# A transformer layer with eight experts: the experts' rows in 63 whole and 9 half units that the chip plans, instead of 80 fixed chunks

## The chip, the cores and the metric

The kernel runs on one core of a Trainium2 chip. The metric is the time of one execution on the device in microseconds (us), lower is better. The kernel before has a median of 3489.76 us over 3 runs (3483.92 to 3495.27).

## What is computed

The layer takes 32 sequences of 512 tokens with 256 features, all in float32:

```python
x = layernorm(x + attention(x))       # 16 heads of 16, softmax over 512 keys, projection, bias
x = layernorm(x + experts(x))
# experts: 16384 tokens, 8 experts, each token goes to its best 2
cap = int(N * K * CF / E)             # 5120 rows at most for one expert
logits = x @ Wg.T
top_v, top_i = top_k(logits, 2); gates = softmax(top_v)
pos = cumsum(onehot(top_i)) - 1; keep = pos < cap
h = rows_of_expert @ W1[e]            # 256 -> 1024
h = gelu(h[:, :512]) * h[:, 512:]
y = h @ W2[e]                         # 512 -> 256
out = segment_sum(gate * y, token)
```

There are 16384 * 2 = 32768 rows to compute, which is 64 times 512. How they fall on the eight experts depends on the data.

## The kernel before

The program has three blocks, one after the other, each ended by a barrier of all engines.

**Attention** (`attention`) goes over the 32 sequences in a software pipeline that is written out in full. Beside the heads it normalises, computes the router's logits, and gives each token two slots in a table in HBM, `expert_rows`: 8 experts times 5120 slots, 260 numbers wide (256 features, and the token's number, its gates and its first expert). POOL scatters the rows into their slots with indirect DMAs (L504). The table was filled before with blank rows, whose token number is far out of range. The running number of rows of each expert is `carry`. When the last iteration is over, ACT and DVE split the weights of expert 0 into a high and a low part (L778, L1022), beside the last scatter.

**Experts** (`experts`) goes over 80 chunks of 512 slots, ten for each expert, full or blank, whatever the data are, in loops of the program (`chunks`). TensorE multiplies float32 as three products of high and low parts. For a chunk:

- SP loads the rows, transposed in four quarters, and their meta data (`load_rows`, five DMAs, L1134 and L1135), two buffers deep. It does so once DVE has turned the rows that lay in the buffer and has read their meta data (`s_turn`, `s_meta`).
- DVE turns the rows (L1280), ACT and DVE split them (L1231, L1286).
- PE computes the hidden products f = 0 to 3 (`hidden`, L1193, 12 matmuls of 512 columns each), and between f = 1 and f = 2 the output products of the chunk before (`output`, L1206, 48 matmuls of 256 columns).
- ACT applies the Gelu (L1235), DVE multiplies (`product`, L1292), ACT and DVE split the result (L1241, L1297), ACT scales the output by the gate (`scale`, L1249), and POOL adds the rows into the result in HBM with four indirect DMAs (L1163).
- DVE reads gate and token out of the meta data (`meta`, L1309 to L1313).

Once per expert, in its second chunk, SP loads the next expert's raw W1 (four DMAs of 256 KB, L226) and W2 (one of 512 KB, L227) into one raw buffer, and POOL splits them (L1176, L1178) into the other of two sets of split weights, `w1_hi`, `w1_lo`, `w2_hi`, `w2_lo` (named stack and w_buf in the trace).

**final_norm** normalises the result, limited by its loads and stores.

Of the kernel before, what the change touches and what calls it, by code (L numbers as in the profile page):

```python
# [10 lines left out]

# [115 lines left out]
def settle(engine, sem):  # L127


    engine.sem_inc(sem, 1)  # L130
# [72 lines left out]
LOADED = 16 * (QUARTERS + 1)  # L203
W_PIECES = 3


class Weights:
# [3 lines left out]
    def __init__(self, stacks, w2_buf, probs, w1, w2):  # L211
# [12 lines left out]
    def load(self, engine, e, s_raw):  # L224
        for a in range(QUARTERS):
            engine.dma_start(self.raw1[a * BLOCK:(a + 1) * BLOCK], self.w1_rows[e, a]).then_inc(s_raw, 16)  # L226
        engine.dma_start(self.raw2, self.w2_rows[e]).then_inc(s_raw, 16)  # L227

    def pieces(self, par):

        return [(self.raw1[:, 0], self.w1_hi[par][0], self.w1_lo[par][0]),
                (self.raw1[:, 1], self.w1_hi[par][1], self.w1_lo[par][1]),
                (self.raw2, self.w2_hi[par], self.w2_lo[par])]


def attention(nc, x, w_qkv, w_proj, b_proj, w_gate, x1_dram, table, stacks, probs, weights):
# [3 lines left out]
    cap = table.shape[0] // EXPERTS  # L240
# [7 lines left out]
    with ExitStack() as ctx:  # L248
# [77 lines left out]
        token = sb("token", [P, TILES])  # L326

# [34 lines left out]
        s_raw = sem("s_raw_a")  # L362
        s_whi, s_wlo = sem("s_whi_a"), sem("s_wlo_a")
# [11 lines left out]
        def _(sp):  # L375
# [8 lines left out]
            def body(it):  # L384
                b = it.b
                for s in range(4):
# [36 lines left out]
                    if s == 3 and it.known and b == n_seq:  # L423
                        sp.wait_ge(s_pv, n_seq * UNITS)
                        weights.load(sp, 0, s_raw)
# [10 lines left out]
            sp.wait_ge(s_fill, 16 * EXPERTS * per)  # L436
# [3 lines left out]
        def _(pool):  # L440
# [25 lines left out]
            pool.wait_ge(s_pad, 2 * GROUPS)  # L466
            pool.wait_ge(s_weights, 64)

            def body(it):
# [26 lines left out]
                if it.on(-2):  # L496
                    pool.wait_ge(s_slot, b - 1)

                    pool.wait_ge(s_fill, (b - 1) * (16 * EXPERTS) if it.filling else 16 * EXPERTS * per)
                    settle(pool, s_waited_pool)  # L500
                    for k in range(TOPK):
                        for t in range(TILES):
                            c = k * TILES + t
                            pool.indirect_dma_start(  # L504
                                table, bass.IndirectOffsetOnAxis(ap=slot[:, c:c + 1], axis=0), row[it.odd][:, t, :], None,
                                bounds_check=table.shape[0] - 1, oob_is_err=False).then_inc(s_scatter, 16)
# [27 lines left out]
        def _(pe):  # L534
# [157 lines left out]
            iterations(pe, n_seq, body)  # L692

        @block.scalar
        def _(act):
# [79 lines left out]
            act.wait_ge(s_raw, LOADED)  # L775
            act.wait_ge(s_cols, n_seq * ALL)
            for raw_w, hi, _ in weights.pieces(0):
                act.copy(hi, raw_w).then_inc(s_whi, 1)  # L778

        @block.vector  # L780
        def _(dve):
# [238 lines left out]
            for i, (raw_w, hi, lo) in enumerate(weights.pieces(0)):  # L1020
                dve.wait_ge(s_whi, i + 1)
                dve.tensor_tensor(lo, raw_w, hi.bitcast(F32), ALU.subtract).then_inc(s_wlo, 1)  # L1022


def experts(nc, table, weights, x1_dram):

    cap = table.shape[0] // EXPERTS
    per = cap // SEQ
    n_chunks = EXPERTS * per
    n_tokens = x1_dram.shape[0]
    assert cap % SEQ == 0 and per % 2 == 0 and EXPERTS % 2 == 0 and EXPERTS > 4 and per > 2
    WIDTH = DIM // QUARTERS  # L1040
    chunk_x = table[:, 0:DIM].rearrange("(n b j) (a c) -> n a j b c", b=SEQ // BLOCK, j=BLOCK, a=QUARTERS)
    chunk_meta = table[:, DIM:ROW].rearrange("(n t p) c -> n p t c", p=P, t=TILES)

    with ExitStack() as ctx:
# [12 lines left out]
        quarters = [sb(f"quarters{i}", [P, SEQ // BLOCK, WIDTH]) for i in range(2)]  # L1057
        meta_rows = [sb(f"meta_rows{i}", [P, TILES, ROW - DIM]) for i in range(2)]
        turned = sb("turned", [P, KT, SEQ])
        x_hi = [sb(f"x_hi{i}", [P, KT, SEQ], F32R) for i in range(2)]  # L1060
        x_lo = [sb(f"x_lo{i}", [P, KT, SEQ], F32R) for i in range(2)]
        w1_hi, w1_lo, w2_hi, w2_lo = weights.w1_hi, weights.w1_lo, weights.w2_hi, weights.w2_lo
# [8 lines left out]
        expert_no = sb("expert_no", [P, 1])  # L1071

        s_rows = [sem(f"s_rows{i}") for i in range(2)]
        s_raw = sem("s_raw")
        s_whi = sem("s_whi")
        s_w = sem("s_w")
# [13 lines left out]
        s_eno = sem("s_eno")  # L1090


        s_waited_sp, s_waited_pool = sem("s_waited_sp_e"), sem("s_waited_pool_e")

        ADDED = 16 * TILES

        class Chunk:


            def __init__(self, e, par, lead, half, odd, last=False):  # L1100
                self.e, self.par, self.lead, self.half, self.odd, self.last = e, par, lead, half, odd, last
                self.n = half * 2 + odd
                self.first = isinstance(half, int) and self.n == 0
                self.final_expert = isinstance(e, int) and e == EXPERTS - 1

        def chunks(engine, body):

            halves = per // 2

            def expert(e, par, final=False):  # L1110
                for odd in range(2):
                    body(Chunk(e, par, True, e * halves, odd))
                with engine.Fori(1, halves - 1 if final else halves) as i:
                    for odd in range(2):
                        body(Chunk(e, par, False, e * halves + i, odd))
                if final:
                    for odd in range(2):
                        body(Chunk(e, par, False, e * halves + halves - 1, odd, last=True))

            expert(0, 0)  # L1120
            expert(1, 1)
            with engine.Fori(1, EXPERTS // 2 - 1) as pair:
                expert(pair * 2, 0)
                expert(pair * 2 + 1, 1)
            expert(EXPERTS - 2, 0)
            expert(EXPERTS - 1, 1, final=True)
# [3 lines left out]
        @block.sync  # L1130
        def _(sp):
            def load_rows(odd, n):
                for a in range(QUARTERS):
                    sp.dma_start(quarters[odd][a * BLOCK:(a + 1) * BLOCK], chunk_x[n, a]).then_inc(s_rows[odd], 16)  # L1134
                sp.dma_start(meta_rows[odd][:], chunk_meta[n]).then_inc(s_rows[odd], 16)  # L1135

            load_rows(0, 0)
            load_rows(1, 1)

            def body(k):  # L1140
                if k.lead and k.odd and not k.final_expert:
                    wait(sp, s_w, k.e * W_PIECES)
                    settle(sp, s_waited_sp)
                    weights.load(sp, k.e + 1, s_raw)
                if not k.last:
                    sp.wait_ge(s_turn, k.n * KT + KT)
                    settle(sp, s_waited_sp)
                    sp.wait_ge(s_meta, k.n + 1)
                    settle(sp, s_waited_sp)
                    load_rows(k.odd, k.n + 2)  # L1150

            chunks(sp, body)
            sp.wait_ge(s_add, n_chunks * ADDED)

        @block.gpsimd
        def _(pool):
            def add_out(buf, n):

                pool.wait_ge(s_scaled, n * TILES + TILES)
                wait(pool, s_add, n * ADDED)  # L1160
                settle(pool, s_waited_pool)
                for t in range(TILES):
                    pool.indirect_dma_start(  # L1163
                        x1_dram, bass.IndirectOffsetOnAxis(ap=token[buf][:, t:t + 1], axis=0), out[buf][:, t, :], None,
                        bounds_check=n_tokens - 1, oob_is_err=False, compute_op=ALU.add).then_inc(s_add, 16)

            def body(k):
                if not k.first:
                    add_out(1 - k.odd, k.n - 1)
                if k.lead and k.odd and not k.final_expert:  # L1170

                    pool.wait_ge(s_raw, k.e * LOADED + LOADED)
                    wait(pool, s_out, k.e * per)
                    settle(pool, s_waited_pool)
                    for i, (raw, hi, lo) in enumerate(weights.pieces(1 - k.par)):
                        pool.tensor_copy(hi, raw).then_inc(s_whi, 1)  # L1176
                        pool.wait_ge(s_whi, k.e * W_PIECES + (i + 1))
                        pool.tensor_tensor(lo, raw, hi.bitcast(F32), ALU.subtract).then_inc(s_w, 1)  # L1178

            chunks(pool, body)  # L1180
            add_out((n_chunks - 1) % 2, n_chunks - 1)

        @block.tensor
        def _(pe):
            def hidden(c, f):

                wait(pe, s_mul, c.n * FT + (f - 1))
                for part in range(2):
                    cols = slice(part * FF + f * P, part * FF + (f + 1) * P)
                    i = 0  # L1190
                    for k in range(KT):
                        for w, xx in ((w1_hi, x_hi), (w1_lo, x_hi), (w1_hi, x_lo)):
                            last = pe.matmul(ps_hid[f % 2][:, part, :], w[c.par][k][:, cols], xx[c.odd][:, k, :],  # L1193
                                             start=i == 0, stop=i == 3 * KT - 1)
# [3 lines left out]
            def output(par, buf, n):  # L1198
# [282 lines left out]
```

## Time and profile before

| | |
|---|---|
| median of 3 runs | 3489.76 us (3483.92 to 3495.27) |
| profiled execution | 3492.51 us |
| its span, from the first to the last instruction | 3490.8 us |
| attention, up to the first row load of the experts | 0 to 2002.18 us |
| experts | 2002.18 to 3389.01 us |
| final norm | 3389.01 to 3490.8 us |
| PE, DVE, ACT, POOL busy, share of the span | 92%, 70%, 61%, 50% |

An instruction's time is its own duration on its engine. Matmuls overlap, so the time of one matmul in a row of them is the distance between starts, and not the duration shown. The value in brackets behind a row of the timeline is the idle time of the engine before it, and what ended it. The execution profiled took 2.75 us more than the median.

### The profile page before, as it was taken

What the parts mean: (1) busy time and instruction counts of PE and PEld (TensorE: products, weight loads), DVE (VectorE), ACT (ScalarE), POOL (GpSimd) and SP (SyncE); (2) the same over time, 40 slices, a digit from 0 to 9 for tenths busy, and PEclk for the clock granted to TensorE, in tenths of its full rate; (3) what the DMA queues carried; (4) which work ended last, traced back from release to release, by engine and by line L of the source; (5) the groups of instructions that cost most, each with busy time, mean ns of one, the idle gap of its engine ahead of it and who ended that gap; (6) DMA issues with size and microseconds to landing.
All of it is one profiled execution on the core that took longest, in us unless ns stands there. A gap on an engine that the chain in (4) does not pass through costs nothing. (4 is left out here: it accounts for less than half of the span.)

```text
span 3490.8 us, 65927 instructions
## 1 busy us (share of the span) xinstructions
PE 3226.1 (92%) x22018; PEld 2115.3 (61%) x22018; DVE 2446.6 (70%) x5673; ACT 2113.1 (61%) x4197; POOL 1755.3 (50%) x1501
## 2 busy tenths in 40 slices
PE   5999999999999999999999599999999999999960
PEld 3444444444444445444444288888888888888850
DVE  4888888888888888888887364545455545454439
ACT  2788888888877787878886444444444444444420
POOL 5356565656556565656562343434353534353334
PEclk7999999999999999999998799999999999999985
DMA  2455555433333333333332244434345434442439
GB/s 87 142 160 173 160 173 160 123 87 98 87 97 82 97 88 98 87 96 91 92 94 65 77 75 63 74 58 77 57 68 78 62 61 62 70 61 43 62 73 338
DMA packets 397883, 339.88 MB, mean 97 GB/s; under 512 B 257720, under 2 KB 315456, under 8 KB 397632
## 3 DMA queue, kind: packets, MB, share of 16 engines
q1 hardware_dynamic: 334656, 252.20, 27.8%
q0 software_dynamic: 58368, 67.74, 11.3%
q10 hardware_dynamic: 4608, 16.78, 1.2%
q8 instruction: 136, 2.23, 0.3%
q14 instruction: 115, 0.94, 0.1%
HBM read 89.92 MB, written 152.17 MB: 69 GB/s over the span
## 5 line engine op out<-in xcount | busy, mean ns | idle before, releaser
L974 DVE TENSOR_REDUCE peak<-ps 128x1 f32<-128x512 f32 x2048 | 1338.5, 683 | 293.0 <-PE ps L654 292.4
L749 ACT ACTIVATE probs<-ps 128x512 f32<-128x512 f32 x2048 | 1124.5, 611 | 173.8 <-PE ps L664 164.9
L1163 POOL DMA_INDIRECT x<-out,token x320 | 501.7, 1568 | 800.0 <-ACT out L1249 669.4
L1193 PE MATMUL ps_hid<-x_hi,stack 128*128 128x512 f32 x2560 | 804.2, 395 | 30.9 <-DVE x_lo L1286 26.3
L664 PE MATMUL ps<-stack 50*128 50x512 f32 x2048 | 786.2, 453 | 3.4 <-DVE peak L974 2.7
L654 PE MATMUL ps<-stack 48*128 48x512 f32 x2048 | 753.8, 446 | 18.9 <-DMA stack<-qk_lo 13.6
L1292 DVE TENSOR_TENSOR hid<-ps_hid,act_in 128x512 f32<-128x512 f32 x320 | 219.1, 689 | 598.0 <-ACT act_in L1235 597.8
L654 PEld LDWEIGHTS ps<-stack 48*128 48x128 f32 x2048 | 336.0, 189 | 466.7 <-issue 223.2
L1193 PEld LDWEIGHTS ps_hid<-x_hi,stack 128*128 128x128 f32 x2560 | 476.5, 188 | 140.3 <-DVE x_lo L1286 26.4
L680 PE MATMUL ps_pv<-probs,v 128*17 128x512 f32 x4096 | 546.9, 606 | 1.2 <-ACT probs L749 1.2
L1193 PE MATMUL ps_hid<-x_lo,stack 128*128 128x512 f32 x1280 | 505.4, 395 | 0.0
L1206 PE MATMUL ps_out<-w_buf,h_hi 128*128 128x256 f32 x2560 | 463.7, 283 | 2.9 <-DVE h_lo L1297 2.9
L504 POOL DMA_INDIRECT expert_rows<-row,slot x256 | 254.9, 996 | 407.9 <-DVE token L954 323.6
L1206 PEld LDWEIGHTS ps_out<-w_buf,h_hi 128*128 128x128 f32 x2560 | 401.8, 189 | 10.1 <-issue 3.3
L1235 ACT ACTIVATE act_in<-ps_hid 128x512 f32<-128x512 f32 x320 | 190.2, 597 | 308.6 <-PE ps_hid L1193 308.6
L664 PEld LDWEIGHTS ps<-stack 50*128 50x128 f32 x2048 | 335.4, 186 | 58.6 <-DVE peak L974 38.7
L1206 PE MATMUL ps_out<-w_buf,h_lo 128*128 128x256 f32 x1280 | 363.1, 284 | 0.0
L488 POOL TENSOR_TENSOR qk<-qk 128x512 f32<-128x512 f32 x128 | 164.0, 1281 | 355.0 <-ACT qk L700 355.0
L1249 ACT ACTIVATE out<-ps_out,gate 128x256 f32<-128x256 f32 x320 | 125.7, 476 | 274.2 <-PE ps_out L1206 274.2
L1193 PEld LDWEIGHTS ps_hid<-x_lo,stack 128*128 128x128 f32 x1280 | 241.1, 188 | 57.0
L1297 DVE TENSOR_TENSOR h_lo<-hid,h_hi 128x512 fp32r<-128x512 f32 x320 | 237.8, 747 | 15.2
L1206 PEld LDWEIGHTS ps_out<-w_buf,h_lo 128*128 128x128 f32 x1280 | 241.9, 189 | 0.0
(136 smaller groups left out, 4095.6 us busy)
## 6 DMA issues: line engine op xcount, KB each, us to landing
stack<-qk_hi SPq DMA_DIRECT2D x1024, 64.0 KB, 2.3
expert_rows<-blank SPq DMA_DIRECT2D x80, 520.0 KB, 4.0
quarters<-expert_rows SPq DMA_DIRECT2D x320, 128.0 KB, 2.7
stack<-qk_lo SPq DMA_DIRECT2D x512, 64.0 KB, 2.3
xs<-in_L_attn_x SPq DMA_DIRECT2D x32, 512.0 KB, 4.3
x<-row SPq DMA_DIRECT2D x32, 512.0 KB, 3.3
fy<-x SPq DMA_DIRECT2D x32, 512.0 KB, 4.6
out<-fz ACTq DMA_DIRECT2D x32, 512.0 KB, 4.7
```

Source lines behind the costliest of these rows:

```text
L504: pool.indirect_dma_start(table, bass.IndirectOffsetOnAxis(ap=slot[:, c:c + 1], axis=0), row[it.odd][:, t, :], None, bounds_check=table.sh ...
L654: pe.matmul(ps[it.bank(("rows", n))][:], q_stack[s][part, h, t * P:(t + 1) * P], k_stack[s][part, h, :], start=True, stop=True).then_inc(s ...
L664: pe.matmul(ps[it.bank(("cols", n))][:], k_stack[g][part, h, t * P:(t + 1) * P], q_stack[g][part, h, :], start=True, stop=True).then_inc(s ...
L680: last = pe.matmul(ps_pv[32 * h:32 * h + HD + 1, :], v[par][:, t, HG * g + h, :], probs[:, (HG * t + h) % RING, :], start=t == 0, stop=t = ...
L749: act.activation(probs[:, j % RING, :], ps[it.bank(("cols", s * UNITS + j))][:], ACT.Exp, scale=SCALE).then_inc(s_exp, 1)
L974: dve.tensor_reduce(peak[s % 2][:, u:u + 1], ps[it.bank(("rows", n))][:], AX.X, ALU.max, negate=True).then_inc(s_max, 1)
L1163: pool.indirect_dma_start(x1_dram, bass.IndirectOffsetOnAxis(ap=token[buf][:, t:t + 1], axis=0), out[buf][:, t, :], None, bounds_check=n_t ...
L1193: last = pe.matmul(ps_hid[f % 2][:, part, :], w[c.par][k][:, cols], xx[c.odd][:, k, :], start=i == 0, stop=i == 3 * KT - 1)
L1206: last = pe.matmul(ps_out[:, t, :], hh[buf][:, f, t * P:(t + 1) * P], w[par][:, f, :], start=i == 0, stop=i == 3 * FT - 1)
L1235: act.activation(act_in[f % 2][:], ps_hid[f % 2][:, 0, :], ACT.Gelu).then_inc(s_gelu, 1)
L1292: dve.tensor_tensor(hid[f % 2][:], ps_hid[f % 2][:, 1, :], act_in[f % 2][:], ALU.mult).then_inc(s_mul, 1)
L1297: dve.tensor_tensor(h_lo[c.odd][:, f, :], hid[f % 2][:], h_hi[c.odd][:, f, :].bitcast(F32), ALU.subtract).then_inc(s_hlo, 1)
```

## The change

The experts' work is cut into units instead of chunks: 63 whole ones of 512 slots and then 9 halves of 256. That is the number that suffices for any distribution of 32768 rows on eight experts. Which slots and which expert's weights belong to a unit is worked out at the end of attention: PE sums `carry` over the partitions, and DVE works out two numbers for each unit (`plan.numbers`: place in the table, expert) and the expert for the gates (`plan.expert`), in some 70 instructions on tiles of up to 544 numbers a partition. A unit without work gets a blank place added behind the table. SP reads a number into a register (`value_load`, a TENSOR_LOAD) ahead of a load of rows or weights.

Since any unit may have another expert than the one before, **W1 and W2 are loaded and split for every unit**. ACT makes the high parts and DVE the low ones, in pieces of 128x1024 between the steps of a unit; POOL only adds rows. The buffers of rows become three. The loops of the program become code written out.

```diff
+class Plan:
+    def __init__(self, sb, n_tokens, cap):
+        self.per = cap // SEQ
+        self.blank = EXPERTS * self.per
+        halves = n_tokens * TOPK // (SEQ // 2) + EXPERTS - 1
+        self.whole = (halves - EXPERTS) // 2
+        self.n_halves = halves - 2 * self.whole
...
+    def rows(self, engine, n):
+        return engine.value_load(self.numbers[0:1, 0, n:n + 1], min_val=0, max_val=last)
+    def weights(self, engine, n):
+        return engine.value_load(self.numbers[0:1, 1, n:n + 1], min_val=0, max_val=EXPERTS - 1)
...
@@ attention, sync @@
-                    if s == 3 and it.known and b == n_seq:
-                        sp.wait_ge(s_pv, n_seq * UNITS)
-                        weights.load(sp, 0, s_raw)
+            sp.wait_ge(s_pv, n_seq * UNITS)
+            sp.wait_ge(s_planned, 2)
+            first = plan.weights(sp, 0)
+            weights.load_w1(sp, first)
+            weights.load_w2(sp, first)
@@ attention, tensor @@
+            pe.matmul(ps_pv[:, 0:EXPERTS], ones[:], carry[:], start=True, stop=True).then_inc(s_total, 1)
@@ attention, scalar @@
-            for raw_w, hi, _ in weights.pieces(0):
-                act.copy(hi, raw_w).then_inc(s_whi, 1)
@@ experts, sync @@
-            def body(k):
-                if k.lead and k.odd and not k.final_expert:
-                    wait(sp, s_w, k.e * W_PIECES)
-                    weights.load(sp, k.e + 1, s_raw)
-                if not k.last:
-                    sp.wait_ge(s_turn, k.n * KT + KT)
-                    sp.wait_ge(s_meta, k.n + 1)
-                    load_rows(k.odd, k.n + 2)
+            for n in range(RING_X):
+                load_rows(n)
+            expert = plan.weights(sp, 1)
+            sp.wait_ge(s_w1, KT)
+            weights.load_w1(sp, expert)
+            for n in range(n_units):
+                if n + RING_X < n_units:
+                    sp.wait_ge(s_turn, n * KT + KT)
+                    sp.wait_ge(s_meta, n + 1)
+                    load_rows(n + RING_X)
+                if n + 2 < n_units:
+                    later = plan.weights(sp, n + 2)
+                    sp.wait_ge(s_w1, (n + 2) * KT)
+                    weights.load_w1(sp, later)
+                if n + 1 < n_units:
+                    sp.wait_ge(s_w2, n + 1)
+                    weights.load_w2(sp, expert)
+                    expert = later
@@ experts, gpsimd: the split of the weights goes @@
-                        pool.tensor_copy(hi, raw).then_inc(s_whi, 1)
-                        pool.tensor_tensor(lo, raw, hi.bitcast(F32), ALU.subtract).then_inc(s_w, 1)
@@ experts, scalar @@
+            for n in range(n_units):
+                more = n + 1 < n_units
+                if more:
+                    high_x(n + 1)
+                gelu(n, 0)
+                gelu(n, 1)
+                high_h(n, 0)
+                if more:
+                    high_w1(n + 1, 0)
+                high_h(n, 1)
+                if more:
+                    high_w1(n + 1, 1)
+                high_w2(n)
+                if n:
+                    scale(n - 1)
+                gelu(n, 2)
+                gelu(n, 3)
+                high_h(n, 2)
+                high_h(n, 3)
@@ experts, vector: as on ACT, with turn and low_x, then @@
+                product(n, 0)
+                product(n, 1)
+                low_h(n, 0)
+                if more:
+                    low_w1(n + 1, 0)
+                low_h(n, 1)
+                if more:
+                    low_w1(n + 1, 1)
+                low_w2(n)
+                meta(n)
+                product(n, 2)
...
```

The two places where instructions move are these. On SP, the loads of one chunk in the middle of an expert before (quarters and meta_rows are the buffers of the rows, probs is the raw buffer of the weights; ISA rows write a register):

```order
L1134 ISA
L1134 DMA quarters<-expert_rows 32x16x64
L1134 ISA
L1134 DMA quarters<-expert_rows 32x16x64
L1134 ISA
L1134 DMA quarters<-expert_rows 32x16x64
L1134 ISA
L1134 DMA quarters<-expert_rows 32x16x64
L1135 ISA
L1135 DMA meta_rows<-expert_rows 128x4x4
```

and now those of one whole unit (the three quarters' and two weights' DMAs left out read like their neighbours):

```order
L256 TENSOR_LOAD plan_numbers
L256 ISA x2
L1258 ISA
L1258 DMA quarters<-expert_rows 32x16x64
...
L1260 ISA
L1260 DMA meta_rows<-expert_rows 128x4x4
L259 TENSOR_LOAD plan_numbers
L259 ISA x2
L228 ISA
L228 DMA probs<-in_L_ffn_W 32x2x1024
...
L231 ISA
L231 DMA probs<-in_L_ffn_W 128x4x256
```

Five loads a chunk have become ten a unit, with two reads of a number into a register ahead of them. On DVE, one chunk before, from the turn of the next rows on:

```order
L1280 STREAM_TRANSPOSE turned<-quarters 128x512 x2
L1286 TENSOR_TENSOR x_lo<-turned,x_hi 128x512 x2
L1292 TENSOR_TENSOR hid<-ps_hid,act_in 128x512 x2
L1297 TENSOR_TENSOR h_lo<-hid,h_hi 128x512 x2
L1309 SCALAR_TENSOR_TENSOR gate_part<-meta_rows,expert_no 128x4
L1312 TENSOR_TENSOR gate<-gate_part,meta_rows 128x4
L1313 COPY token<-meta_rows 128x4
L1292 TENSOR_TENSOR hid<-ps_hid,act_in 128x512 x2
L1297 TENSOR_TENSOR h_lo<-hid,h_hi 128x512 x2
```

and one whole unit now:

```order
L1397 STREAM_TRANSPOSE turned<-quarters 128x512 x2
L1403 TENSOR_TENSOR x_lo<-turned,x_hi 128x512 x2
L1417 TENSOR_TENSOR hid<-ps_hid,act_in 128x512 x2
L1422 TENSOR_TENSOR h_lo<-hid,h_hi 128x512
L1408 TENSOR_TENSOR stack<-probs,stack 128x1024
L1422 TENSOR_TENSOR h_lo<-hid,h_hi 128x512
L1408 TENSOR_TENSOR stack<-probs,stack 128x1024
L1412 TENSOR_TENSOR w_buf<-probs,w_buf 128x1024
L1431 SCALAR_TENSOR_TENSOR gate_part<-meta_rows,plan_expert 128x4
L1434 TENSOR_TENSOR gate<-gate_part,meta_rows 128x4
L1435 COPY token<-meta_rows 128x4
```

Three subtractions of 128x1024 stand ahead of the reading of the meta data, for which SP waits.

## Rows read from the trace of the kernel before

**Rows 1.** The page: span, and busy time of each engine.

```profile
span 3490.8 us, 65927 instructions
...
PE 3226.1 (92%) x22018; PEld 2115.3 (61%) x22018; DVE 2446.6 (70%) x5673; ACT 2113.1 (61%) x4197; POOL 1755.3 (50%) x1501
```

**Rows 2.** Windows: stretch, length, busy times, granted clock, DMA share, GB/s.

```profile
2009.83:3363.77 1353.94, 1349.37 (x7632) 1175.88 (x7632) 707.24 (x1201) 583.90 (x1112) 574.57 (x356) 1.00 0.42 64
...
2603.15:2620.14 16.99, 16.99 (x98) 14.86 (x97) 8.20 (x17) 7.34 (x14) 6.25 (x5) 1.00 0.43 62
...
2688.00:2705.00 17.00, 17.00 (x98) 14.80 (x98) 8.64 (x17) 7.45 (x14) 6.28 (x5) 1.00 0.72 139
...
3363.77:3388.00 24.23, 7.47 (x48) 7.29 (x48) 1.98 (x3) 3.29 (x7) 9.73 (x7) 0.73 0.12 13
```

**Rows 3.** Timeline of one chunk: start, us, engine, line, what, count, [idle before].

```profile
2605.93 0.40 PE L1206 MATMUL ps_out<-w_buf,h_hi 128*128 128x256 f32 x2
...
2606.29 0.40 PE L1206 MATMUL ps_out<-w_buf,h_hi 128*128 128x256 f32 x2
...
2609.08 0.17 DVE L1313 COPY token<-meta_rows 128x4 uint32<-128x4 uint32 x1
...
2609.50 1.92 SPq L1134 DMA_DIRECT2D quarters<-expert_rows  x4
...
2611.97 1.57 ACT L1249 ACTIVATE out<-ps_out,gate 128x256 f32<-128x256 f32 x4 [3.87 <-PE ps_out L1206]
...
2615.30 0.69 DVE L1292 TENSOR_TENSOR hid<-ps_hid,act_in 128x512 f32<-128x512 f32 x1 [6.05 <-ACT act_in L1235]
```

**Rows 4.** SP's queue in the second chunk of an expert.

```profile
2694.31 1.91 SPq L1134 DMA_DIRECT2D quarters<-expert_rows  x4
...
2697.16 1.82 SPq L226 DMA_DIRECT2D probs<-in_L_ffn_W  x4
...
2699.16 0.39 SPq L227 DMA_DIRECT2D probs<-in_L_ffn_W  x1
```

**Rows 5.** DMA issues, 2050 to 3360 us: count, KB each, median us to landing.

```profile
quarters<-expert_rows SPq DMA_DIRECT2D x304, 128.0 KB, 2.7
...
probs<-in_L_ffn_W SPq DMA_DIRECT2D x24, 256.0 KB, 4.5
...
probs<-in_L_ffn_W SPq DMA_DIRECT2D x6, 512.0 KB, 6.4
```

**Rows 6.** Timeline of the end of attention and the start of the experts.

```profile
1983.53 0.19 DVE L911 TENSOR_TENSOR pos_all<-count,ps 128x32 f32<-128x32 f32 x1 [0.30 <-PE ps L641]
...
1985.26 1.04 ACT L778 CAST w_buf<-probs 128x1024 fp32r<-128x1024 f32 x1
...
1985.73 2.35 DVE L1022 TENSOR_TENSOR stack<-probs,stack 128x1024 fp32r<-128x1024 f32 x2
...
1996.75 0.97 POOL L504 DMA_INDIRECT expert_rows<-row,slot  x1 [0.30 <-issue]
...
2002.18 1.92 SPq L1134 DMA_DIRECT2D quarters<-expert_rows  x4
...
2009.83 1.22 PE L1193 MATMUL ps_hid<-x_hi,stack 128*128 128x512 f32 x2 [26.33 <-DVE x_lo L1286]
...
2019.84 0.60 ACT L1235 ACTIVATE act_in<-ps_hid 128x512 f32<-128x512 f32 x1 [0.81 <-PE ps_hid L1193]
```

**Rows 7.** Timeline of the end of the experts.

```profile
3369.63 0.63 PE L1206 MATMUL ps_out<-w_buf,h_hi 128*128 128x256 f32 x2
...
3370.27 0.63 PE L1206 MATMUL ps_out<-w_buf,h_hi 128*128 128x256 f32 x2
...
3373.84 0.29 PE L1206 MATMUL ps_out<-w_buf,h_lo 128*128 128x256 f32 x1
...
3376.61 1.55 POOL L1163 DMA_INDIRECT x<-out,token  x1 [8.69 <-ACT out L1249]
...
3378.47 1.55 POOL L1163 DMA_INDIRECT x<-out,token  x1 [0.30 <-issue]
```

More of the change, by code:

```diff
@@ L1019, in _, with planned, then @@
             iterations(dve, n_seq, body)
[L1020 to L1037, printed above, removed]
+            def planned(ins):
+                ins.then_inc(s_plan, 1)
+                step[0] += 1
+            def then():
+                dve.wait_ge(s_plan, step[0])
@@ new lines, in _ @@
+            total = work([P, EXPERTS])
+            reached = work([P, EXPERTS, per])
+            own_chunks = work([P, EXPERTS])
+            own_steps = work([P, EXPERTS])
+            small = work([P, EXPERTS])
+            small_at = work([P, EXPERTS])
+            upto = work([P, 2 * EXPERTS, EXPERTS])
+            ends = work([P, 2 * EXPERTS])
+            ended = work([P, plan.n_chunks, EXPERTS])
+            start = work([P, plan.n_chunks])
+            chunk_e = work([P, plan.n_chunks])
@@ new lines, in _ @@
+            then()
+            planned(dve.tensor_reduce(own_chunks, reached, AX.X, ALU.add))
+            then()
+            planned(dve.tensor_tensor(small, own_steps, own_chunks, ALU.subtract))
+            then()
+            for e in range(EXPERTS):
+                planned(dve.tensor_copy(upto[:, e, 0:e + 1], own_chunks[:, 0:e + 1]))
+                planned(dve.tensor_copy(upto[:, EXPERTS + e, 0:e + 1], small[:, 0:e + 1]))
+            planned(dve.scalar_tensor_tensor(small_at, number[:], float(per), own_chunks, ALU.mult, ALU.add))
@@ new lines, in _ @@
+            dve.tensor_scalar(plan.numbers[:, 1, 0:W], chunk_e[:, 0:W], EXPERTS - 1.0, None, ALU.min).then_inc(s_planned, 1)
+            then()
+            planned(dve.tensor_reduce(start, ended, AX.X, ALU.max))
+            planned(dve.scalar_tensor_tensor(place, chunk_e, float(per), chunk_no[:], ALU.mult, ALU.add))
+            then()
+            planned(dve.tensor_tensor(place, place, start, ALU.subtract))
+            then()
+            planned(dve.tensor_scalar(place, place, float(plan.blank), None, ALU.min))
@@ L1089, in experts, with cols, scaled_before, added_before @@
         s_add = sem("s_add")
[L1090 to L1126, printed above, removed]
+        def cols(n):
+            return plan.tiles(n) * P
+        def scaled_before(n):
+            return plan.tiles_before(n)
+        def added_before(n):
+            return 16 * plan.tiles_before(n)
         block = ctx.enter_context(nc.Block())
@@ L1155, in _ @@
+            sp.wait_ge(s_add, added_before(n_units))
         @block.gpsimd
         def _(pool):
[L1157 to L1162, printed above, removed]
+            for n in range(n_units):
+                pool.wait_ge(s_scaled, scaled_before(n + 1))
+                wait(pool, s_add, added_before(n))
+                for t in range(plan.tiles(n)):
```

374 lines of the change are left out of this document (225 added, 149 removed).

## The prediction

> **What bounds the kernel now.** I read the page first, for the engines' shares: PE is busy for 92% of the span [rows 1]. The windows then show the experts' stage apart. From its first matmul at 2009.83 us to the end of the last hidden products at 3363.77 us, PE is busy for 1349.37 of 1353.94 us at a granted clock of 1.00 [rows 2], while DVE has 707 and ACT 584 us of work. A chunk takes 16.99 us, of which DVE is busy for 8.20 and ACT for 7.34. So this stage is bound by PE, and there are 80 chunks of it. The timeline shows what a chunk is made of: its output products start at 2605.93, and three matmuls of 256 columns take 0.36 us, so 0.12 us each [rows 3]. 48 of these take 5.76 us, which leaves 11.2 us for the 48 hidden ones of 512 columns, 0.234 us each. A chunk whose rows belong to nobody costs PE as much as a full one. The attention and the final norm are not touched, and I leave them at their times.
>
> **Fewer units: 288.8 us less.** 63 whole units take the place of the first 63 of 80 chunks. If PE stays the bound, each of the 17 chunks that go gives back 16.99 us: 17 x 16.99 = 288.8 us. The half units have to be added to that, below.
>
> **Does the new work fit into a whole unit?** Each now splits 1.5 MB of weights. ACT gets three copies of 128x1024, of 1.04 us each, 3.1 us in all; DVE three subtractions, two of which took 2.35 us, so 3.6 us in all [rows 6]. ACT comes to 10.5 us and DVE to 11.8 us of 16.99. The order matters more than the sum. Both engines do the splits while PE works on the output products. ACT stands idle for 3.87 us there before it scales, and DVE for 6.05 us before its next product [rows 3]. The 3.1 and 3.6 us fit into these gaps, so I cost them at nothing in a whole unit. If that cover went, each microsecond over it would cost 62 us. DVE's reading of the meta data, which ends at 2609.25 (8.9 us after the chunk's start, with 24 hidden matmuls ahead of the output at 2605.93), moves to 12.5 us, because the three subtractions are ahead of it.
>
> **The loop of loads.** That reading is what SP waits for, and behind SP's wait now stand the weights of the next units too. There is one raw buffer, so the weights go round in a loop, for W2 in this order: the reading ends; SP issues 0.25 us later (2609.25 to 2609.50, [rows 3]); a number is read into a register, r; five loads of rows are issued in 2.5 us; a second number, r; W1's four loads go 2.0 us ahead of W2's; W2 lands 6.4 us after its issue [rows 4, 5]; ACT's copy 1.0, DVE's subtraction 1.2, the reading 0.55, and 0.1 for the handings over. That makes 14.0 us + 2r. By W1, landing after 4.5 us with three copies and a Gelu half's split behind it, the sum is the same within 0.2 us.
>
> No row shows r. Nearest from below is SP's issue of one load, 0.39 us [rows 4]; even nothing is possible. From above, a whole small load lands after 2.7 us [rows 5]. I take r = 0.8, nearer to an issue, since four bytes have no queue of packets ahead. The Trainium skill, page "DMA: Bandwidth & Descriptors", section "Latency and other measured facts", gives a floor of about 600 ns for such a read; by that floor the loop would be 0.4 us shorter and the whole time about 3 us. With mine the loop is 15.6 us. In a whole unit that is under 16.99 us, so PE hides it with 1.4 us to spare; r above 1.5 us, or as much more in the landing, would end that.
>
> **The half units are bound by the loop: 122.6 us more.** PE needs 72 matmuls of 256 columns, 72 x 0.12 = 8.6 us. The splits and loads of weights don't get smaller, and the loop stays at 15.6 us. So in the halves PE waits for DVE's low part of the weights and for products queued behind it. Counted from the end of the whole units' hidden products: the first half unit, whose weights were loaded under a whole one, reads its meta data after 10.7 us (an estimate: 12.5 less what the narrower steps save); six loops of 15.6 us are 93.6; one without rows to load is 15.6 - 2.5 - 0.8 = 12.3; one with W2 alone is 0.25 + 6.4 + 2.75 less some queue, 9.1; product and splits 2.0; the last output products, 24 matmuls at the lower clock, 5.1. Together 133 us. Before, the output products ended 10.4 us after the hidden ones (3363.77 to 3374.13, [rows 7]). So 133 - 10.4 = 122.6 us are added. PE's pauses also lower its clock: after the wait at the end three matmuls take 0.64 instead of 0.36 us, mean clock 0.73 [rows 2, 7]. A whole half unit at that rate, 1.2 GHz, is 72 x 0.213 = 15.3 us, just under the loop; I cost it at nothing.
>
> **The start: 3.0 us more.** The plan has some 30 dependent steps on DVE. In the routing ten such steps lie between 1983.53 and 1985.73 [rows 6], 0.22 us each, so 6.6 us. Four of them are on 544 numbers, and a product on 512 takes 0.69 us [rows 3], so 2 us more; 34 small copies without a wait between them I put at 0.1 us each. That is about 12 us from 1985.7, so to 1998. Beside it POOL scatters until 1997.7 and the block ends at 2002.18 [rows 6]. So the plan is hidden with a small margin; without it up to 12 us would show. ACT's and DVE's splits of the first weights move behind the barrier: two copies and two subtractions, 3.3 us with their overlap. The first matmul comes 7.65 us after the first row load there [rows 6], and most of that is waiting for the rows, so they are hidden. The first read adds r = 0.8 us. Then SP has three sets of rows to issue, 3 x (2.5 + 0.8), before W1 of unit 1, which lands at about 2019; ACT's third Gelu, at 2019.84 before [rows 6], comes at 2022.6 instead, for 2.2 us. POOL makes three small index tiles at the very start of the program, before it has anything to split; I cost them at nothing, and at some tenths if nothing covers them.
>
> **The end: 4.5 us less.** The last unit has two tiles, not four: 0.8 us less scaling of 1.57 [rows 3], and two adds fewer at 1.86 us from start to start [rows 7].
>
> **The sum.** -288.8 + 122.6 + 3.0 - 4.5 = -167.7 us. The span goes from 3490.8 to 3323 us, the profiled time from 3492.5 to 3325 us. The median of before is 2.75 us under that execution, so I say **3322 us**.
>
> **The rivals.**
> - *As above*: 60%, 3295 to 3360 us by itself (r from 0 to 1.5 and as much in the landing; at the clock's lower level some microseconds per half unit).
> - *Loads are quicker than the rows say, and the halves run at PE's pace.* Nine times 8.64 and the tails are 86 us instead of 133, so 3275 us. For it: the landings in rows 5 were measured with five loads just ahead and adds beside them, and half units have half of these. Against it: W2 is always behind W1, and DVE alone has at least 8.20 / 2 + 3.6 = 7.7 us of work in a half unit. 10%. The Trainium skill, same page, section "Anatomy of one DMA", fits 2.0 us + bytes / 436e3 for a DMA of GpSimd alone, which would be 3.2 us for W2. By that rule the halves' loop is 12.4 us and the time about 3299 us; row 5's 6.4 us speaks against it.
> - *The loop is over 17 us and binds the whole units too.* The DMA engines go from a share of 0.43 to 0.72 in the window with one load of weights [rows 2], and now every unit is such a window. Each microsecond of loop over 16.99 costs 62 us there and 7 more in the halves; a loop of 18 us gives 3322 + 62 x 1.0 + 7 x 2.4 = 3401 us. Against it: the 6.4 us were measured in such windows. 25% from 3340 to 3480 us.
> - *Slower.* The same mechanism decides the sign at a loop of 19.4 us, where 62 x 2.4 + 7 x 3.8 = 175 us eat the gain: W2 would have to land after 10.2 instead of 6.4 us, or r be at its upper bound of 2.7. With 20 us: 3539 us. 5%.
> - That half units cost PE as much as whole ones is excluded by the output products, which run at 256 columns in half the time.
>
> **How the numbers follow.** The forecast is the likeliest case. The range reaches down to the quick loads, 3275, and up to a loop of 18 us, 3400; the upper part of the third case and the fourth stay out, with what lies below. A measurement of this kernel can tell about 0.3%, 10 us, from no change. Faster by more: 94%; slower by more: 5%; within: 1%.
>
> **What would show it.** Right: 63 periods of 16.9 to 17.0 us with clock 1.00; a third stretch of some 130 us with PE half idle, released by DVE's products; in it 15 to 16 us from one row load of SP to the next; SP's W2 landing at 6 to 7 us; first matmul 27 us after the end of routing, not more. Wrong: periods of over 17 us in the whole units with ACT's copy of probs released by a DMA (rivals three and four), or 9 to 10 us in the halves (rival two).

## The result and the profile after

| | before | after |
|---|---|---|
| median, same chip | 3490.16 us (3483.92 to 3495.27, 4 runs) | 3410.75 us (3407.68 to 3413.28, 4 runs) |
| ratio, 95% interval | | 0.977 (0.9755 to 0.9784) |
| span profiled | 3490.8 | 3410.2 |
| first experts' matmul | 2009.83 | 2013.95 |
| from there to the end of the last output products | 1364.3 | 1279.6 |
| from there to the final norm's first load | 14.9 | 8.4 |
| final norm | 101.8 | 108.3 |

The change gains 2.3%, 79 us, which is less than half of the 168 us that were forecast. It was forecast at 3322 us, with a range up to 3400, so it lies 11 us outside. The profiled executions differ by 80.6 us: the first matmul comes 4.1 us later, the stage is 84.7 us shorter, the wait behind it 6.5 us shorter, and the norm 6.5 us longer. The loss against the forecast is in the experts' stage. The windows of after, of whole units and of half units (the columns as in [rows 2]):

```profile
2050.00:3050.00 1000.00, 947.50 (x5319) 809.81 (x5318) 632.25 (x997) 552.14 (x940) 367.27 (x223) 1.00 0.70 147
3150.00:3290.00 140.00, 95.23 (x650) 93.64 (x648) 70.14 (x156) 61.82 (x133) 33.84 (x22) 0.83 0.55 119
```

PE, which had no pause in a chunk before [rows 2], is idle for 5% of the whole units though its clock is 1.00. From one of ACT's copies of W2 to the next pass 18.04 us, the mean over 60, where a chunk took 16.99. In the halves a unit takes 16.2 to 18.0 us. The waits from 2050 to 3050 us (engine, tile, line, who is waited for: us in total, times, longest) say who holds it:

```profile
DVE stack L1408 <- ACT stack L1341: 271.8, 55, 6.1
ACT stack L1341 <- DMA probs<-in_L_ffn_W: 257.1, 55, 5.9
...
PE ps_hid L1302 <- DVE hid L1417: 52.3, 49, 2.1
...
ACT w_buf L1345 <- DMA probs<-in_L_ffn_W: 2.1, 4, 1.0
```

In every unit ACT's first copy of W1 waits for the weights, 4.7 us on average; DVE's low part waits for ACT, and PE for the product that is queued behind. It is W1 that is late: W2 is waited for in 4 units only. The timeline of one unit of after shows the loop (as [rows 3]; some rows of SP, ACT, DVE and POOL):

```profile
2500.26 0.16 DVE L1435 COPY token<-meta_rows 128x4 uint32<-128x4 uint32 x1
...
2500.54 1.55 POOL L1288 DMA_INDIRECT x<-out,token  x1 [10.42 <-ACT out L1363]
2501.22 2.02 SPq L1258 DMA_DIRECT2D quarters<-expert_rows  x4
...
2504.56 1.81 SPq L228 DMA_DIRECT2D probs<-in_L_ffn_W  x4
...
2506.13 1.69 POOL L1288 DMA_INDIRECT x<-out,token  x1 [0.30 <-issue]
...
2506.55 0.39 SPq L231 DMA_DIRECT2D probs<-in_L_ffn_W  x1
...
2512.96 1.05 ACT L1341 CAST stack<-probs 128x1024 fp32r<-128x1024 f32 x1 [4.55 <-DMA probs<-in_L_ffn_W]
...
2515.72 1.05 ACT L1345 CAST w_buf<-probs 128x1024 fp32r<-128x1024 f32 x1 [0.23 <-DMA probs<-in_L_ffn_W]
...
2518.39 0.16 DVE L1435 COPY token<-meta_rows 128x4 uint32<-128x4 uint32 x1
...
2519.34 1.92 SPq L1258 DMA_DIRECT2D quarters<-expert_rows  x4
```

The four parts of the loop, as means over 53 whole units, beside the terms of the forecast (the last one is what is left of its sum):

| part of the loop | forecast, us | measured, us |
|---|---|---|
| end of DVE's reading of the meta data (its copy of the token) to the rows' first issue: SP reads a number | 0.25 + 0.8 | 0.81 |
| rows' first issue to W1's first issue | 2.5 + 0.8 | 3.57 |
| W1's first issue to ACT's first copy | 1.5 + 4.5 | 8.07 (7.08 to 9.34) |
| ACT's first copy to the end of the meta reading | 5.25 | 5.6 |
| sum | 15.6 | 18.05 |

### The profile page after: what moved, and what is told of

Read it like the earlier page. It is cut to its first block and busy times, and to the rows that moved or that the text cites. A ratio compares the mean times of both kernels' runs of the same rounds, so it can differ in the third digit from the quotient of the medians.

```text
span 3410.2 us, 63298 instructions
## 1 busy us (share of the span) xinstructions
PE 3043.8 (89%) x21035; PEld 1947.2 (57%) x21035; DVE 2537.0 (74%) x5828; ACT 2217.3 (65%) x4280; POOL 1618.4 (47%) x1412
## 5 line engine op out<-in xcount | busy, mean ns | idle before, releaser
L1302 PE MATMUL ps_hid<-x_hi,stack 128*128 128x512 f32 (+1 forms) x2304 | 707.8, 391 | 131.5 <-DVE hid L1417 101.4
L1302 PE MATMUL ps_hid<-x_lo,stack 128*128 128x512 f32 (+1 forms) x1152 | 446.9, 388 | 0.0
L1408 DVE TENSOR_TENSOR stack<-probs,stack 128x1024 fp32r<-128x1024 f32 x144 | 175.8, 1222 | 354.4 <-ACT stack L1341 354.4
L1316 PE MATMUL ps_out<-w_buf,h_hi 128*128 128x256 f32 x2160 | 387.5, 281 | 1.9 <-DVE h_lo L1422 1.9
L1341 ACT CAST stack<-probs 128x1024 fp32r<-128x1024 f32 x144 | 150.9, 1048 | 345.9 <-DMA probs<-in_L_ffn_W 324.4
L1316 PEld LDWEIGHTS ps_out<-w_buf,h_hi 128*128 128x128 f32 x2160 | 336.7, 189 | 7.5 <-issue 2.1
L1316 PE MATMUL ps_out<-w_buf,h_lo 128*128 128x256 f32 x1080 | 303.5, 281 | 0.0
L1417 DVE TENSOR_TENSOR hid<-ps_hid,act_in 128x512 f32<-128x512 f32 (+1 forms) x288 | 184.2, 653 | 122.1 <-ACT act_in L1349 121.5
L1349 ACT ACTIVATE act_in<-ps_hid 128x512 f32<-128x512 f32 (+1 forms) x288 | 160.6, 574 | 136.9 <-PE ps_hid L1302 136.4
L750 ACT COPY qk<-ps 128x512 f32<-128x512 f32 x256 | 137.5, 589 | 132.5 <-PE ps L640 128.5
```

The costliest lines, as they stand in the source:

```text
L1302: last = pe.matmul(ps_hid[f % 2][:, part, 0:cols(n)], w[n % 2][k][:, w_cols], xx[n % 2][:, k, 0:cols(n)], start=i == 0, stop=i == 3 * KT - 1)
L1316: last = pe.matmul(ps_out[:, t, :], hh[n % 2][:, f, t * P:(t + 1) * P], w[n % 2][:, f, :], start=i == 0, stop=i == 3 * FT - 1)
L1408: dve.tensor_tensor(w1_lo[n % 2][k], raw1[:, k], w1_hi[n % 2][k].bitcast(F32), ALU.subtract).then_inc(s_w1, 1)
L1417: dve.tensor_tensor(hid[f % 2][:, 0:cols(n)], ps_hid[f % 2][:, 1, 0:cols(n)], act_in[f % 2][:, 0:cols(n)], ALU.mult).then_inc(s_mul, 1)
```

## The experiments

The theories after the result: **the loop**, as in the table, binds every unit (the rows in front of the weights, DVE's meta reading behind the subtractions, one raw buffer); or the **work of splitting** on ACT and DVE doesn't fit; or the **traffic** of 1.5 MB more a unit is too much, whatever the order. The first four kernels ran on a chip where before takes 3490.97 us. Three of them leave a part of the work out: the planned places, the later loads of weights, most of the adds. They measure that part and are no candidates.

### Weights first

```diff
             for n in range(n_units):
-                if n + RING_X < n_units:
-                    sp.wait_ge(s_turn, n * KT + KT)
-                    sp.wait_ge(s_meta, n + 1)
-                    load_rows(n + RING_X)
                 if n + 2 < n_units:
...
                     expert = later
+                if n + RING_X < n_units:
+                    sp.wait_ge(s_turn, n * KT + KT)
+                    sp.wait_ge(s_meta, n + 1)
+                    load_rows(n + RING_X)
```

> Theory L (the loop of the single raw buffer binds: reading of the meta data, rows' loads, weights' loads, landing, splits): with the weights' loads issued ahead of the rows' and no longer behind the meta data, the loop shrinks from 18.0 to some 13 us, the whole units go back to 17.0 us (-64 us) and the halves from 17.2 to about 13 us (-30 us): 3315 us. Theory D (the 16 DMA engines are at their throughput, share 0.7): the order changes nothing, 3410 us. Theory S (the splits on ACT and DVE cost the time, whenever the weights come): 3410 us.

Measured: **3293.71 us (3290.71 to 3305.57), 0.9444 (0.9422 to 0.9466) of before.** One moved statement gives 117 us more than the change alone. W1's load now follows its own last subtraction and not the meta reading. The window and the waits:

```profile
2050.00:3050.00 1000.00, 1000.00 (x5689) 870.18 (x5689) 684.29 (x1067) 596.34 (x1008) 380.95 (x236) 1.00 0.80 156
```

```profile
DVE hid L1417 <- ACT act_in L1349: 288.5, 177, 2.5
...
DVE stack L1408 <- ACT stack L1341: 10.0, 59, 0.3
```

PE has no pause in 1000 us and the copy doesn't wait for a DMA at all. A whole unit takes 16.88 us, a half one 10.8 to 12.1. All the bytes and all the splits are still there, in less time (156 GB/s against 147), so neither the amount of traffic nor splitting held the units. This is the version to keep.

### Without the reads

```diff
-        return engine.value_load(self.numbers[0:1, 0, n:n + 1], min_val=0, max_val=last)
+        return n if n < self.whole else 2 * self.whole + (n - self.whole)
...
-        return engine.value_load(self.numbers[0:1, 1, n:n + 1], min_val=0, max_val=EXPERTS - 1)
+        return n % EXPERTS
```

> Rows and weights are taken from fixed places (unit n, expert n modulo 8) instead of planned ones, so no number is read into a register, and each token's rows meet other weights. L: two reads of 0.75 us go from the loop, 18.0 becomes 16.5 us, hidden in whole units (-64 us), 10 us less in the halves, 2 at the start: 3335 us. D and S: 3405 to 3410 us.

Measured: 3327.1 us (2 runs), 0.9532 (0.9513 to 0.9551). From the token's read to SP's issue pass 0.08 instead of 0.81 us, from the rows' issue to W1's 2.51 instead of 3.57. So the first read costs 0.73 us and the second 1.06 us. Without both the whole units run at 16.91 us, the halves at 15.3 to 17.1. The loop, 16.8 us by its parts (W1 to copy 8.62), is just at PE's pace: it was over by so little that 1.8 us decide 84 us. The fixed places bring one more difference: blank rows are among them, and from 2050 to 3050 us the adds move 25.0 MB in 59 units instead of 28.8 in 56. W1 didn't land sooner by that, since W1 to copy is 8.62 us against 8.07.

### Weights loaded once

The loads of W1 and W2 in SP's loop go; ACT waits only for the first.

```diff
-                act.wait_ge(weights.s_raw1, (n + 1) * W1_LOADED)
+                act.wait_ge(weights.s_raw1, W1_LOADED)
...
-                act.wait_ge(weights.s_raw2, (n + 1) * W2_LOADED)
+                act.wait_ge(weights.s_raw2, W2_LOADED)
```

> The raw weights are loaded once, for unit 0, and split again in every unit; the later loads are left out, so all units use the first expert's weights. L and D: whole units at 17.0 us, halves at the pace of DVE, under 10 us: about 3280 us. S: 3400 us.

Measured: 3282.64 us (2 runs), 0.9405 (0.9386 to 0.9424). Whole units 16.88 us, most halves 9.4. With all splits and no loads PE sets the pace: the theory of splitting falls, and costing the splits at nothing in a whole unit was right. It also bounds what any order of loads can give: 11 us less than weights first.

### Few adds

```diff
-                wait(pool, s_add, added_before(n))
-                for t in range(plan.tiles(n)):
+                if n % 8 == 7:
+                    wait(pool, s_add, 16 * (n // 8))
                     pool.indirect_dma_start(
-                        x1_dram, bass.IndirectOffsetOnAxis(ap=token[n % 2][:, t:t + 1], axis=0), out[n % 2][:, t, :], None,
+                        x1_dram, bass.IndirectOffsetOnAxis(ap=token[n % 2][:, 0:1], axis=0), out[n % 2][:, 0, :], None,
```

> Only every eighth unit adds its first tile of output into the result, the other adds are left out. If the adds' traffic is what lengthened the landing of the weights over what was seen before: landings back at 4.5 (W1) and 6.4 us (W2), the loop at 16 to 16.5 us, 3335 us. If the landing is long by the order of SP's own loads: within 10 us of 3405 us.

Measured: 3355.99 us (3348.22 and 3363.76), 0.9615 (0.9587 to 0.9643): between the two cases of the expectation. Whole units take 17.31 us, W1 to copy 7.42 instead of 8.07. So the adds account for 0.73 of the 1.05 us over the 16.99 us of before, and not for all. What the rest is, the trace's view of W1's line says (time from issue to landing of one set of four loads, first before, then after):

```profile
DMA to landing us min/median/max: 3.3/4.4/5.6
```

```profile
DMA to landing us min/median/max: 4.5/5.4/6.9
```

ACT waits for the last of the four, issued 1.5 us after the first: 2506.05 + 6.9 is 2512.95, when the copy starts. The last of the four also takes longest: before, they land 3.3, 3.9, 4.9 and 5.6 us after their issues. The longest of four is 5.5 us in the mean of the six sets before, 6.5 over 20 units after, and 5.7 with few adds. So of the 2.0 us by which this landing was missed, 1.0 is the longest against the median, which before shows already, and 0.8 to 1.0 the adds. Before, SP issued W1 at 2697.16 and POOL's adds began at 2698.94, beside its last load; after, the add at 2500.54 comes 4 us before the loads, and the fourth at 2506.13 is issued beside W1's last one. Whether that matters, the DMA view shows for the stretch from W1's first issue to its last landing (queue: packets, MB, share of the 16 engines' time, which can exceed 100% where packets overlap; q1 carries SP's loads, q0 POOL's adds; first before, from 2697.16 to 2704.28 us, then after, from 2504.56 to 2512.96):

```profile
q1 hardware_dynamic: 1695, 1.48, 103.9%
```

```profile
q1 hardware_dynamic: 2203, 1.71, 88.1%
q0 software_dynamic: 370, 0.35, 26.0%
```

Before, the adds' packets moved nothing while W1 was in flight, and the add of 2698.94 landed after 7.2 us instead of the usual 3.7: it stood behind the loads. After, the adds' packets are among W1's. The engines are full in that stretch, a share of 1.14 at 244 GB/s, and have a share of 0.32 in the rest of the unit, up to 2522.61. So the landing is long by what stands in that burst, and not by the sum of the traffic.

### Two raw buffers

The following kernels ran on chips that grant less clock in the attention, a mean of 0.91 over its time against 0.97 (before takes 3761.94 us, in the last set 3752.7); the ratios, and the time from the first matmul to the start of the last one of the stage, can be compared: 1279.4 us after, 1168.6 with weights first.

The weights are again asked for ahead of the rows, now two units ahead.

```diff
-        raw1, raw2 = weights.raw1, weights.raw2
+        raw_b = sb("raw_b", [P, KT * 2 * FF + FT * DIM])
+        raw1 = [weights.raw1, raw_b[:, 0:KT * 2 * FF].rearrange("p (k f) -> p k f", k=KT)]
+        raw2 = [weights.raw2, raw_b[:, KT * 2 * FF:].rearrange("p (k d) -> p k d", k=FT)]
...
+            load_rows(0)
+            expert = plan.weights(sp, 1)
+            load_w1(1, expert)
+            load_w2(1, expert)
+            for n in range(1, RING_X):
                 load_rows(n)
...
+                if n + 2 < n_units:
+                    expert = plan.weights(sp, n + 2)
+                    sp.wait_ge(s_w1, (n + 1) * KT)
+                    load_w1(n + 2, expert)
+                    sp.wait_ge(s_w2, n + 1)
+                    load_w2(n + 2, expert)
                 if n + RING_X < n_units:
```

> Two raw buffers, and a unit's weights are asked for two units ahead of their split. Theory L: the loads of weights leave the loop, whole units 16.9 us, halves at the pace of DVE as with weights loaded once, 9.4 us: 3285 us. If the halves at 11.2 us with the weights' loads first were already bound by the DMA engines' throughput: they stay there, 3294 us.

Measured: 3562.83 us (3535.69 to 3568.74), 0.9435 (0.9382 to 0.9487); stage 1166.2 us. No gain that can be told from weights first in the whole: where PE has no pause, as in the whole units, a deeper buffer has nothing to hide. But the stretches differ. The last halves take 9.4 us each, as the expectation's theory L had it, and from the 65th unit's first Gelu to the start of the last matmul pass 84.2 us, against 92.2 and 89.8 in the two traces with weights first. The start gives it back: the second unit's rows are issued at 2280.50, behind the second unit's weights, DVE waits 7.5 us for them, and from the first matmul to the third unit's first Gelu pass 40.8 us instead of 36.8 and 37.2. Two raw buffers with those rows ahead of the weights were not tried.

### Meta data early

SP's order stays, rows first.

```diff
                 low_h(n, 0)
+                meta(n)
                 if more:
                     low_w1(n + 1, 0)
...
                 low_w2(n)
-                meta(n)
```

> Only DVE's reading of the meta data moves, ahead of the three subtractions of weights; SP's order stays. L: the rows' loads go out while the weights are still split, W1's loop becomes landing 8.1 + copies and subtractions 3.9 + about 1 us, under 16.9: whole units 16.9 us, halves about 12 us, 3305 us. If what mattered in the run with the weights' loads first was only SP's order: 3380 us or more.

Measured: 3585.13 us (3573.65 to 3599.52), 0.9522 (0.9474 to 0.957); stage 1185.6 us, whole units 16.91, halves 11.0 to 15.1. The same loop, cut at its other end, gives most of the same gain. So it is the loop and not something in SP's order by itself.

### The final norm: other places in memory

The norm's code is the same and takes 6.5 us more. Two kernels try where its data or the plan's lie. One is the change with the plan's tiles padded to 1024 bytes a partition:

```diff
-        self.numbers = sb("plan_numbers", [P, 2, self.n_units], U32)
+        both = sb("plan_both", [P, 256], U32)
+        self.numbers = both[:, 0:2 * self.n_units].rearrange("p (a n) -> p a n", a=2)
-        self.expert = sb("plan_expert", [P, self.n_units])
+        self.expert = sb("plan_expert", [P, 256])[:, 0:self.n_units]
```

> The plan's two tensors are made 1024 bytes a partition each, not 576 and 288, so the buffers allocated behind them start at multiples of 1024 bytes of where they were. Theory P (placement in the on-chip memory lengthens the final norm from 101.8 to 108.2 us by its loads and stores): 3404 us, norm back at 102 us. Rival (something else, such as the place of the tensors in HBM): 3410 us, norm at 108 us.

Measured: 3668.41 us (3646.52 to 3673.19), 0.9723 (0.9673 to 0.9773); whole units 18.05, norm 108.3 us. No effect. The other is the kernel before with the longer table of the change:

```diff
-    table = nc.dram_tensor("expert_rows", [EXPERTS * cap, ROW], F32).ap()
+    table = nc.dram_tensor("expert_rows", [EXPERTS * cap + SEQ, ROW], F32).ap()[0:EXPERTS * cap]
```

> The kernel before, with one thing of the change: the table expert_rows is 512 rows longer, so what lies behind it in HBM lies elsewhere. It computes all. Theory P (the final norm's 108 us instead of 102 comes from where things lie in HBM): last output of the experts to the end takes the change's time, the norm 108 to 110 us, and all else is unchanged, so +6 us against before. Theory T (it comes from something else, such as the chip's state or the program's length): the norm stays at 101 to 103 us, within 0.3% of before. I give T 60%: padding other tensors left the changed kernel's norm at 108.

Measured: 3746.81 us (3730.52 to 3776.71), 0.9977 (0.994 to 1.0013); norm 101.8 us. So the longer table doesn't do it either. The norm's loads and stores, before and after:

```profile
fy<-x SPq DMA_DIRECT2D x32, 512.0 KB, 4.6
out<-fz ACTq DMA_DIRECT2D x32, 512.0 KB, 4.7
```

```profile
fy<-x SPq DMA_DIRECT2D x32, 512.0 KB, 5.6
out<-fz ACTq DMA_DIRECT2D x32, 512.0 KB, 5.8
```

Each DMA lands 1 us later. By the DMA view it is the loads' packets that take longer: 49.9% of 101.8 us before and 52.0% of 108.3 after, where the stores' take 42 us in both. All eleven kernels with the units have a norm of 105 to 111 us, and both without them 101.8. It comes with the change; by what, stays open. The places of other tensors, and the loops that became code written out, were not tried by themselves.

### The first load of weights behind the barrier

```diff
-            first = plan.weights(sp, 0)
-            weights.load_w1(sp, first)
-            weights.load_w2(sp, first)
...
+            first = plan.weights(sp, 0)
+            weights.load_w1(sp, first)
+            weights.load_w2(sp, first)
             for n in range(RING_X):
                 load_rows(n)
```

> The first unit's raw weights are loaded at the start of the experts' block instead of beside the last scatter. If their traffic delays the scatter's end, and with it the barrier: SP's first instruction after it comes 4.5 us after the last scatter's start as before the change, not 8.3 less the read's 0.8 us. The first matmul then waits for the weights: 3 to 6 us more in all, 3414 us. If the traffic does not matter: the barrier stays, 3418 us.

Measured: 3680.87 us (one run; before 3742 to 3781, the padded kernel 3668.41). From the start of the last scatter to SP's first load behind the barrier pass 6.6 us; in the padded kernel, which loads early, 9.6, with one read of a number in either. So with the early load the block ends some 3 us later, which fits a scatter that lands later; the trace has no landing for it. But the first matmul comes 21.7 us after the last scatter instead of 17.0: paying 3 us for early weights is right.

### All cures together, and weights first again

Two raw buffers with the meta data early, as in the two diffs above; beside it the first experiment's kernel unchanged.

> All cures in one: SP asks for weights first and two units ahead, into two raw buffers, and DVE reads the meta data ahead of the three subtractions. It computes all. By the theory of the loop, whole units already run at PE's pace of 16.9 us with the weights first alone, so nothing is left there; what is left is in the nine halves, 10.8 to 12.1 us each against 8.6 of PE at full clock. If the loop of loads still holds them, two raw buffers and early meta data bring them towards 9.5 to 10, 10 to 20 us less in all than with the weights first alone. If the traffic or DVE holds them (two raw buffers alone gained nothing measurable), the time is within 0.3% of the weights first alone. I take the second, 65%: ratio to before equal to that of the kernel with weights first beside it.

> The kernel with the weights first once more, beside the one with all cures and on the same chip. Theory L: 0.944 of before again where the chip gives full clock, whole units of 16.9 us; on a chip that grants less clock in the attention about 0.946, as the attention weighs more. Theory of chance (its first gain was of one chip): over 0.96.

Measured: both cures 3553.05 us (3539.83 to 3591.59), 0.9444 (0.9395 to 0.9494); weights first again 3535.03 us (3522.82 to 3547.59), **0.9397 (0.935 to 0.9444)**. The single move holds on another chip. All cures together aren't better, and their stage is longer, 1184.1 against 1166.6 us. The waits of the half units, from 3370 to 3470 us, show a wait that my expectation lacked (the second is two raw buffers alone, from 3345 to 3445 us):

```profile
DVE gate_part L1440 <- DMA x<-out,token: 17.6, 5, 5.0
```

```profile
DVE gate_part L1440 <- DMA x<-out,token: 3.0, 1, 3.0
```

Read early, the meta data need the buffer of tokens before POOL's adds of two units back have landed, and DVE's subtractions and products queue behind that wait. With the meta data early alone it was there too, 20.7 us in 6 waits from 3355 to 3460 us. Of the 17.5 us, 4.5 lie before the third unit's first Gelu, nearly as many as with two raw buffers alone; that the wait makes the other 13 is not shown.

## Why the prediction was wrong on size

- **Fewer units, 288.8 us: right in kind.** With weights first the whole units run at 16.88 us, PE's pace, and the gain is there. In the change each of 62 takes 1.05 us more than 16.99, 65 us.
- **Splits at nothing: right.** Without loads the whole units ran at PE's pace with every split in them.
- **The loop of loads, 14.0 us + 2r: this step failed.** Its structure and order were right, and the three experiments that took a step out of it (weights first, without the reads, meta data early) brought the whole units to 16.9 us. The reads were nearly right, 0.73 and 1.06 us for 0.8 each. The Trainium skill, page "DMA: Bandwidth & Descriptors", section "Latency and other measured facts", gives about 600 ns as a floor, and both lie above it. The term that was mis-sized is W1's landing, 4.5 us, which should have been 6.5. The row in [rows 5] is a median over four loads, while ACT waits for the last. And that row came from loads that were ahead of the adds. In the forecast DVE's meta reading moves by 3.6 us and SP's loads with it, and I didn't ask what they then meet: the adds. I took it as comfort that by W1 the sum is the same within 0.2 us; it meant two loops with 1.4 us to spare, and W1's was the one that bound. W2's went over too: it landed after 7.8 us in the mean instead of 6.4, 0.6 us before ACT's copy of it starts, and by W2 the measured loop is 0.8 + 3.6 + 2.2 + 7.8 + 3.1 = 17.5 us. A right size for W1 alone would not have given 15.6.
- **Half units, 122.6 us.** Bound by the loop, as said; the loop, from W1's first issue to the next one's, is 17.2 us in the mean instead of 15.6, 11 us over seven. With 3 us in the last stretch that makes the halves 14 us dearer.
- **The start, 3.0 us.** The plan is hidden, its last piece at 1997.1 us to 1997.3 as against 1998. But the first matmul is 4.1 us late where 0.8 was forecast: with the early load of weights the block ends later, 3 us by the experiment. I had counted its issue and not its traffic.
- **The end, -4.5 us.** It gave -6.5. **The final norm, 0:** +6.5, unexplained.
- The sum: 65 + 14 + 3.3 - 2.0 + 6.5 = 87 us, which is the distance from the forecast span of 3323 to 3410.2 us.
- **The rivals.** The third one happened, with the mark that it was to be known by: periods over 17 us and ACT's copy of probs released by a DMA. At a loop of 18 us it gave 3401 us; the norm and the start, 6.5 and 3.3 us over the forecast, are about what it lacks to 3410.75. Its 25% was too low: 1.4 us of cover is little on a sum with a landing of 4.5 or 6.4 us in it. The second is excluded. The Trainium skill, page "DMA: Bandwidth & Descriptors", section "Anatomy of one DMA", fits 2.0 us + bytes / 436e3 for GpSimd's DMAs, by which W2 would land after an estimated 3.2 us. On SP's queue this trace doesn't agree: W2's median from 2050 to 3050 us is 7.9, and still 6.3 with few adds.

## What to carry to other kernels

When a change makes a loop of load, use and release run every unit, write the loop down and compare it with the bounding engine's period; a sum that fits by a tenth is not hidden. For a buffer filled by several DMAs take the landing of the last one issued, here also the longest, and not the median, and from a stretch with the traffic that the new order gives. And look at what the freeing wait stands behind: here a queue asked for rows that had three buffers before weights that had one, and putting the scarce buffer's load first was worth more than the whole change.

## What the runs showed of the hardware

- A read of a number from SBUF into SP's registers, with its two instructions, costs 0.73 us when SP has just been released and 1.06 us between two groups of loads.
- 256 KB loads beside indirect adds land later: the longest of four took 6.5 us against 5.7 with almost no adds. Adds issued beside the last of such loads moved under 0.01 MB while these were in flight, in all six cases of before, and the first of them landed after 6.5 to 7.5 us instead of 3.7. Adds issued up to 4 us ahead of the loads moved 0.35 MB among them in the unit shown. With 1.5 MB of loads beside the last scatter, the block ended 3 us later.
- The DMA engines carried 156 to 158 GB/s at a share of 0.75 to 0.80 while PE had no pause. In the change the mean share was 0.70 with PE idle for 5%, since the DMA engines were full while W1 was in flight (1.14) and mostly idle in the rest of the unit (0.32).
